# Joining two 64-row products into one 128-row product in the last inner tile of a shared feed-forward layer

## Chip, cores and metric

One core of one Trainium2 chip runs the whole program. The time is device microseconds of one execution. Before the change three runs took 1123.83, 1128.89 and 1127.62 us; the median is 1127.62 us.

## What is computed

Two residual steps on x of shape (4, 2048, 256), that is 8192 tokens of 256 channels. The first is a dynamic convolution over 31 taps, the second a feed-forward layer made of routed experts (16 experts, the best 2 for each token) and of a shared layer that every token passes. The change lies in the shared layer:

```python
SHARED_FF = 704
shared = jax.nn.silu(x @ shared_w_gate.T) * (x @ shared_w_up.T) @ shared_w_down.T
shared = shared * jax.nn.sigmoid(x @ shared_gate_w.T)
...
out = expert_out + shared
...
x = x + _layernorm(_L0_ffn_ref(_layernorm(x, axis=-1), ...), axis=-1)
```

The 704 inner channels are five tiles of 128 and one of 64.

## The kernel before, in words

The program has five blocks, one behind the other: `attention`, `routing`, `shared_and_scatter`, `experts` and `shared_and_combine`. Below, **stage 1** is `shared_and_scatter` (from about 435 us of the span), **stage 2** is `experts`, **stage 3** is `shared_and_combine` (from about 877 us to the end).

The shared layer is the class `Shared`. Its 16 chunks of 512 tokens are split between stage 1 and stage 3, 8 chunks each (`SHARED_CHUNKS`). A chunk walks six inner tiles, m = 0 to 5 (`FT` = 6). For one tile:

- TensorE, `gate_up`: 12 products of 512 columns (6 for m = 5, whose 64 gate and 64 up rows share one bank). Each 32-bit operand is held as a high and a low part, so every product is made of three: high x high, high x low, low x high.
- ScalarE, `silu`, then VectorE, `gated` (tile `hf`, the hidden values), then ScalarE again (tile `hh`, the high part), then VectorE, `hidden_low` (tile `hl`, the low part: hf minus hh).
- TensorE, `down`: for each of four groups of 128 tokens the three products hh x dh, hh x dl, hl x dh, 256 columns each (`dh`, `dl`: high and low part of the down weights). The contraction runs over the tile's rows: 128, and 64 (`FL`) in the tile m = 5. All six tiles of a chunk are summed up in one pair of banks.

`products` writes TensorE's order out by hand: `gate_up` of tile m + 2 (for the last two tiles that of the next chunk) stands ahead of `down` of tile m. So `down` of m = 5 stands between `gate_up` of tiles 1 and 2 of the next chunk. In the last chunk of a stage it is TensorE's last work there.

What stands around it: `leave` (ScalarE, L870) takes the finished chunk out of the banks, in stage 1 to DRAM. Also in stage 1, GpSimd scatters token rows with 128 indirect DMAs (L985). In stage 3 GpSimd gathers two expert rows for each token (L1271, 16 indirect DMAs a chunk) and works out the layer norm's scales (`scales`, L1278 to L1284) between them. VectorE adds expert rows and shared rows (`sums`, L1344 to L1355) at fixed places in its chunk: the sums of one half of the tokens (v = 1) of a chunk at m = 1 and 2 of the next, those of the other half at m = 4 and 5. ScalarE normalizes (L1302), VectorE adds the residual (L1362).

Of the kernel before, what the change touches and what calls it, by code (L numbers as in the profile page):

```python
# [7 lines left out]
F32 = mybir.dt.float32  # L8
# [3 lines left out]
ALU = mybir.AluOpType  # L12
# [4 lines left out]
P = 128  # L17
BATCH, SEQ, C = 4, 2048, 256
# [13 lines left out]
FF, E, MF = 704, 16, 128  # L32
FT = 6
FL = FF - (FT - 1) * P
# [786 lines left out]
class Shared:  # L821
# [67 lines left out]
    def hidden_low(self, ve, i, q, m):  # L889
        f, k, g = self.size(m), m % 2, (m + FT * q) % 4  # L890
        ve.wait_ge(self.s["hh_ok"], (self.base + i) * FT + m + 1)
        self.nc.vector.tensor_tensor(self.hl[0:f, g], self.hf[0:f, k], self.hh[0:f, g].bitcast(F32), ALU.subtract  # L892
                                     ).then_inc(self.s["hl_ok"], 1)

    def gate_up(self, pe, i, q, m):
# [14 lines left out]
    def down(self, pe, i, q, m):  # L910
        g, f = (m + FT * q) % 4, self.size(m)
        pe.wait_ge(self.s["hl_ok"], (self.base + i) * FT + m + 1)
        for t in range(4):
            o = self.pb[4 + 2 * q + t // 2][:, (t % 2) * C:(t % 2 + 1) * C]
            for j, (a, w) in enumerate(((self.hh, self.dh), (self.hh, self.dl), (self.hl, self.dh))):
                ins = self.nc.tensor.matmul(o, a[0:f, g, t * P:(t + 1) * P], w[0:f, m, :],  # L916
                                            start=(m == 0 and t % 2 == 0 and j == 0), stop=(m == FT - 1 and j == 2),
                                            skip_group_check=True)
        if m == FT - 1:
            ins.then_inc(self.s["dn_full"], 1)  # L920

# [126 lines left out]
def experts(nc, sems, eh, el, yt, ynt_d, first_d, xg_d, yg_d, ident, ones, block_expert, pb):  # L1048
    NBK = NBLK + 1
    with ExitStack() as ctx:  # L1050
# [64 lines left out]
        def _(pe):  # L1115
# [37 lines left out]
            def down(b, r):  # L1153
# [6 lines left out]
                ins.then_inc(s["y_full"], 1)  # L1160
            load_experts(0)
            steps(pe, lambda n, r: parts(n, r, (2, turn_x), (-1, turn_h), (1, gate_up), (-2, down), (2, find)), enter)

        @block.scalar
# [242 lines left out]
def _layouts(i):  # L1407
    import numpy as np
    taps = i["L0_attn_w_lin"].reshape(HEADS, KS, C)
    ring = np.concatenate([taps, taps[:, KS - 1:]], 1)[:, [(k - 1) % J for k in range(2 * J)]]  # L1410
    ring = ring.reshape(HEADS, 2 * J, HS, NG, HC).swapaxes(3, 4).reshape(HEADS, 2 * J, C)
    wd = ring.transpose(2, 0, 1).reshape(CC, P, HEADS, 2 * J).transpose(1, 0, 2, 3)
    g = np.concatenate([i["L0_ffn_gate_w"], i["L0_ffn_shared_gate_w"], np.zeros((GW - E - 1, C), "f")], 0)
    gw = g.T.reshape(CC, P, GW).transpose(1, 0, 2)
    gate, up = i["L0_ffn_shared_w_gate"], i["L0_ffn_shared_w_up"]
    rows = [a[m * P:(m + 1) * P] for m in range(FT) for a in (gate, up)]
    wsh = np.concatenate(rows, 0).T.reshape(CC, P, 2 * FF).transpose(1, 0, 2)
    dn = np.concatenate([i["L0_ffn_shared_w_down"].T, np.zeros((FT * P - FF, C), "f")], 0)
    wdn = dn.reshape(FT, P, C).transpose(1, 0, 2)
    gu = i["L0_ffn_w_gate_up"].reshape(E, CC, P, 2 * MF).transpose(0, 2, 1, 3).reshape(E, P, CC * 2 * MF)  # L1420
    we = np.concatenate([gu, i["L0_ffn_w_down"]], 2)
    named = dict(x=i["L0_attn_x"], wd=wd, gw=gw, wsh=wsh, wdn=wdn, we=we)
    return {k: np.ascontiguousarray(v) for k, v in named.items()}
# [13 lines left out]
```

## Time and profile before

| | |
|---|---|
| median of three runs | 1127.62 us (1123.83 to 1128.89) |
| span of the profiled execution | 1124.2 us (its own time is given as this span alone) |
| TensorE matmul busy | 961.3 us, 86% |
| VectorE / ScalarE / GpSimd busy | 801.2 / 574.0 / 488.8 us |
| mean granted TensorE clock | 0.933 of 2.4 GHz |
| chain that ended last | GpSimd 13%, issue 4%, TensorE 3%, others about 1% each |

How to read it: busy shares are means over stages with different limits, so the span is cut into stages first. TensorE's records overlap, because a product is listed with its whole passage through the array; what one product costs in a stream is the distance between starts of neighbours. In the chain of waits GpSimd stands first, and all of that lies in stage 3.

### The profile page before, as it was taken

The page shows a single profiled execution, that of the slowest core. Times are in us where ns is not written, and L with a number is a line of the kernel's source. Part 1 is how long each engine was busy: PE and PEld are TensorE (multiplying, and loading weights), DVE is VectorE, ACT ScalarE, POOL GpSimd, SP SyncE. Part 2 cuts the span into 40 slices and gives each one's busy share as a digit, 9 for nine tenths or more (in the row PEclk, how much of TensorE's full clock was granted, in tenths as well). Part 3 has the DMA queues.
Part 4 walks back from the last instruction along what each step waited for, and adds up shares of the span by engine and source line. Part 5 has one row for each costly group of instructions (what it writes and reads, how often), then busy time and mean ns, then how long its engine had stood idle before and what let it go on. Part 6 is the DMA issues. An engine that isn't in the chain of part 4 may idle for free. (4 is left out here: it accounts for less than half of the span.)

```text
span 1124.2 us, 28049 instructions
## 1 busy us (share of the span) xinstructions
PE 961.3 (86%) x9192; PEld 842.2 (75%) x9193; DVE 801.2 (71%) x2066; ACT 574.0 (51%) x1309; POOL 488.8 (43%) x726
## 2 busy tenths in 40 slices
PE   5997898998899505999999789999999899898881
PEld 4776787776788504888888678999898687777671
DVE  5887997787999694445444368788788378777665
ACT  5993446897254412444444345555555345444442
POOL 4322556220455342776776300000000568787774
PEclk9999998998999556999999889999999899999995
DMA  4333688532578438566665355555555546655553
GB/s 136 113 95 84 184 239 257 164 113 59 147 207 249 155 122 263 182 204 195 205 224 181 95 168 175 168 169 176 169 169 158 158 141 192 187 183 166 167 165 108
DMA packets 188966, 188.16 MB, mean 167 GB/s; under 512 B 55120, under 2 KB 169936, under 8 KB 188752
## 3 DMA queue, kind: packets, MB, share of 16 engines
q1 hardware_dynamic: 173088, 149.25, 44.2%
q0 software_dynamic: 12288, 33.57, 9.1%
q10 hardware_dynamic: 3504, 4.20, 1.2%
q8 instruction: 53, 0.87, 0.3%
q14 instruction: 33, 0.27, 0.1%
HBM read 100.81 MB, written 86.14 MB: 166 GB/s over the span
## 5 line engine op out<-in xcount | busy, mean ns | idle before, releaser
L985 POOL DMA_INDIRECT sorted_rows<-yr,sl x128 | 137.8, 1077 | 76.7 <-issue 38.0
L1271 POOL DMA_INDIRECT cy<-expert_rows,csl x128 | 139.0, 1086 | 45.3 <-issue 44.1
L606 PE MATMUL bank<-xbd,am 128*32 128x68 f32 x4096 | 138.5, 304 | 10.6 <-DMA xbd<-xn_scratch 4.7
L606 PEld LDWEIGHTS bank<-xbd,am 128*32 128x32 f32 x4096 | 122.4, 128 | 18.7 <-issue 10.5
L1264 POOL MEMSET czero<- 128x4 f32 x1 | 0.1, 101 | 241.8 <-POOLq L1050 241.8
L887 DVE TENSOR_TENSOR s_hf<-s_sg,bank 128x512 f32<-128x512 f32 (+1 forms) x48 | 33.0, 688 | 89.8 <-ACT s_sg L862 89.8
L1144 PE MATMUL bank<-eh,xh 128*128 x288 | 94.7, 329 | 0.4 <-DVE xl L1188 0.4
L1188 DVE TENSOR_TENSOR xl<-bank,xh 128x256 fp32r<-128x256 f32 x144 | 61.1, 424 | 40.8 <-ACT xh L1170 33.4
L1170 ACT ACTIVATE xh<-bank 128x256 fp32r<-128x256 f32 x144 | 55.3, 384 | 65.5 <-PE bank L1120 65.2
L407 DVE TENSOR_TENSOR am<-probs,mask 128x512 f32<-128x512 f32 x128 | 80.0, 687 | 8.4 <-ACT probs L501 7.5
L1144 PE MATMUL bank<-el,xh 128*128 x288 | 82.5, 287 | 0.0
L1144 PE MATMUL bank<-eh,xl 128*128 x288 | 82.4, 286 | 0.0
L864 ACT ACTIVATE c_hh<-c_hf 128x512 fp32r<-128x512 f32 (+1 forms) x48 | 30.4, 632 | 98.5 <-DVE c_hf L887 98.5
L916 PE MATMUL bank<-dh,c_hh 128*128 128x256 f32 (+1 forms) x192 | 57.7, 300 | 25.1 <-DVE c_hl L892 25.1
L322 POOL TENSOR_TENSOR rstd<-mv,eps 128x2 f32<-128x2 f32 (+1 forms) x68 | 14.1, 208 | 147.8 <-DVE mv L397 90.1
L1120 PE MATMUL bank<-ident,xg 128*128 128x128 f32 x288 | 57.4, 282 | 24.1 <-issue 12.5
L905 PE MATMUL bank<-c_yh,gh 128*128 128x512 f32 x176 | 71.8, 408 | 6.3 <-DVE c_yl L879 6.3
L515 ACT ACTIVATE av<-av,shift,rstd 128x256 f32<-128x256 f32 x64 | 35.0, 594 | 79.9 <-POOL shift L327 79.9
L905 PE MATMUL bank<-s_yh,gh 128*128 128x512 f32 x176 | 71.5, 406 | 4.5 <-DVE s_yl L879 4.5
L348 POOL TENSOR_TENSOR x<-av,xr 128x256 f32<-128x256 f32 x64 | 46.9, 754 | 62.5 <-ACT yn L524 59.2
L905 PE MATMUL bank<-c_yl,gh 128*128 128x512 f32 x176 | 70.5, 401 | 0.0
L905 PE MATMUL bank<-s_yl,gh 128*128 128x512 f32 x176 | 70.5, 400 | 0.0
(196 smaller groups left out, 3133.1 us busy)
## 6 DMA issues: line engine op xcount, KB each, us to landing
xg<-sorted_rows SPq DMA_DIRECT2D x144, 128.0 KB, 2.1
expert_rows<-yo SPq DMA_DIRECT2D x144, 128.0 KB, 1.8
xbd<-xn_scratch SPq DMA_DIRECT2D x128, 72.0 KB, 2.3
xt<-x SPq DMA_DIRECT2D x32, 256.0 KB, 3.0
xn_scratch<-xn SPq DMA_DIRECT2D x64, 128.0 KB, 2.7
xr<-x SPq DMA_DIRECT2D x32, 256.0 KB, 3.5
x_scratch<-x SPq DMA_DIRECT2D x32, 256.0 KB, 3.6
yn_scratch<-yn SPq DMA_DIRECT2D x32, 256.0 KB, 3.7
```

Of the source, the lines that this page charges most:

```text
L348: nc.gpsimd.tensor_tensor(x2[:, q, t], av[:, q, t], xr[:, q, t], ALU.add).then_inc(s["x2_ok"], 1)
L407: nc.vector.tensor_tensor(am[:, q, g], probs[:, bass.ds(i * CB, CB), g, None, :].to_broadcast([P, CB, 2, J]), mask[:, None].to_broadcast([ ...
L515: nc.scalar.activation(av[:, q, t], av[:, q, t], ACT.Identity, scale=rstd2[:, q, t:t + 1], bias=shift2[:, q, t:t + 1]).then_inc(s["z_ok"], 1)
L606: ins = nc.tensor.matmul(pso[q][t][J * b:J * b + J, g * MW:(g + 1) * MW], am[:, q, g, e, side], xbd[:, q, e + side, :, g], start=(g == 0 a ...
L905: ins = self.nc.tensor.matmul(self.pb[2 * k + half][:], w[:, c, col:col + P], y[:, q, c, :], start=(j == 0), stop=(j == 5))
L916: ins = self.nc.tensor.matmul(o, a[0:f, g, t * P:(t + 1) * P], w[0:f, m, :], start=(m == 0 and t % 2 == 0 and j == 0), stop=(m == FT - 1 a ...
L985: nc.gpsimd.indirect_dma_start(out=xg_d, out_offset=bass.IndirectOffsetOnAxis(ap=sl[:, q, t, u, k:k + 1], axis=0), in_=yr[:, t, u], in_off ...
L1120: ins = nc.tensor.transpose(px[r % 2][:, c * P:(c + 1) * P], xg[:, r, c * P:(c + 1) * P], ident[:])
L1144: ins = nc.tensor.matmul(pg[r % 2][:, 0:2 * MF], a[:, r % 2, c * P:(c + 1) * P], w[:, bass.ds(e, 1), c * C:(c + 1) * C], start=(j == 0), s ...
L1170: nc.scalar.activation(xh[:, r % 2], px[r % 2][:, 0:C], ACT.Copy).then_inc(s["xh_ok"], 1)
L1188: nc.vector.tensor_tensor(xl[:, r % 2], px[r % 2][:, 0:C], xh[:, r % 2].bitcast(F32), ALU.subtract).then_inc(s["xl_ok"], 1)
L1271: nc.gpsimd.indirect_dma_start(out=y[:, v, k, j], out_offset=None, in_=yg_d, in_offset=bass.IndirectOffsetOnAxis(ap=sl[:, v, k, j:j + 1], ...
```

## The change

In the tile m = 5 `hidden_low` writes the low part not to rows 0 to 63 of `hl` but to rows 64 to 127 of `hh`, below the high part. The host puts the last 64 rows of the down weights a second time where zeros were, so that rows 64 to 127 of `dh` hold the same weights as rows 0 to 63. One product over 128 rows then gives hh x dh + hl x dh; the product hh x dl over 64 rows remains, and comes first.

```diff
     def hidden_low(self, ve, i, q, m):
...
-        self.nc.vector.tensor_tensor(self.hl[0:f, g], self.hf[0:f, k], self.hh[0:f, g].bitcast(F32), ALU.subtract
+        low = self.hl[0:f, g] if m < FT - 1 else self.hh[FL:2 * FL, g]
+        self.nc.vector.tensor_tensor(low, self.hf[0:f, k], self.hh[0:f, g].bitcast(F32), ALU.subtract
...
     def down(self, pe, i, q, m):
...
-            for j, (a, w) in enumerate(((self.hh, self.dh), (self.hh, self.dl), (self.hl, self.dh))):
-                ins = self.nc.tensor.matmul(o, a[0:f, g, t * P:(t + 1) * P], w[0:f, m, :],
-                                            start=(m == 0 and t % 2 == 0 and j == 0), stop=(m == FT - 1 and j == 2),
-                                            skip_group_check=True)
+            terms = ((self.hh, self.dh, f), (self.hh, self.dl, f), (self.hl, self.dh, f))
+            if m == FT - 1:
+                terms = ((self.hh, self.dl, FL), (self.hh, self.dh, 2 * FL))
+            for j, (a, w, rows) in enumerate(terms):
+                ins = self.nc.tensor.matmul(o, a[0:rows, g, t * P:(t + 1) * P], w[0:rows, m, :],
+                                            start=(m == 0 and t % 2 == 0 and j == 0),
+                                            stop=(m == FT - 1 and j == len(terms) - 1), skip_group_check=True)
...
-    dn = np.concatenate([i["L0_ffn_shared_w_down"].T, np.zeros((FT * P - FF, C), "f")], 0)
+    dn = np.concatenate([i["L0_ffn_shared_w_down"].T, i["L0_ffn_shared_w_down"].T[FF - FL:]], 0)
```

TensorE's order in stage 1 at the end of a chunk, `down` of m = 5, the first of the four token groups with its neighbours, before (bank3 belongs to `gate_up`, bank4 takes the `down` products; the column at the end is the output's shape):

```order
L905 MATMUL bank3<-s_yl,gh 128x512
L905 MATMUL bank3<-s_yh,gl 128x512
L916 MATMUL bank4<-dh,s_hh 128x256
L916 MATMUL bank4<-dl,s_hh 128x256
L916 MATMUL bank4<-dh,s_hl 128x256
```

and with the change, the first two token groups:

```order
L906 MATMUL bank3<-s_yl,gh 128x512
L906 MATMUL bank3<-s_yh,gl 128x512
L920 MATMUL bank4<-dl,s_hh 128x256
L920 MATMUL bank4<-dh,s_hh 128x256
L920 MATMUL bank4<-dl,s_hh 128x256
```

Each of the four token groups goes from three products, all over 64 rows, to two: `dl` over 64 rows, then `dh` over 128. So `down` of m = 5 goes from 12 products of one height to 8 whose height changes at every step. Nothing ahead of it or behind it moves.

VectorE's order around the same place, before (the 64-row tile is m = 5; `el` are expert weights), and with the change:

```order
L887 TENSOR_TENSOR s_hf<-s_sg,bank2 64x512
L1032 TENSOR_TENSOR el<-eraw,eh 128x768
L892 TENSOR_TENSOR s_hl<-s_hf,s_hh 64x512
```

```order
L887 TENSOR_TENSOR s_hf<-s_sg,bank2 64x512
L1036 TENSOR_TENSOR el<-eraw,eh 128x768
L893 TENSOR_TENSOR s_hh<-s_hf,s_hh 64x512
```

The low part now goes into `s_hh`; the place in the order and the shape stay.

## Rows read from the trace of the kernel before

**Rows 1.** Windows by stage: us, busy us (instructions) by engine, clock, DMA share, GB/s.

```profile
435.20:632.64 197.44, 197.41 (x1104) 170.10 (x1104) 88.44 (x151) 87.88 (x147) 137.82 (x128) 0.98 0.60 196
...
876.60:1106.10 229.50, 204.38 (x1104) 173.00 (x1104) 164.32 (x413) 99.98 (x187) 173.37 (x211) 0.96 0.55 169
1106.10:1124.20 18.10, 0.00 (x0) 0.00 (x0) 8.22 (x24) 5.58 (x12) 4.21 (x13) 0.52 0.38 123
```

**Rows 2.** Waits, whole span: us in total, times, longest us.

```profile
PE bank L916 <- DVE c_hl L892: 25.1, 12, 7.7
...
POOL crstd L1278 <- DVE cmv L1355: 17.4, 3, 8.8
...
PE bank L905 <- DVE s_yl L879: 4.5, 1, 4.5
```

**Rows 3.** Timeline of TensorE, stage 1, boundaries of equal height: start, us, line, tiles.

```profile
461.72 0.39 PE L905 MATMUL bank<-s_yh,gl 128*128 128x512 f32 x1
461.95 0.28 PE L916 MATMUL bank<-dh,s_hh 128*128 128x256 f32 x1
...
463.26 0.28 PE L916 MATMUL bank<-dh,s_hl 128*128 128x256 f32 x1
463.38 0.40 PE L905 MATMUL bank<-s_yh,gh 128*128 128x512 f32 x1
```

**Rows 4.** Timeline of TensorE, the first `down` of m = 5 and its neighbours.

```profile
465.94 0.40 PE L905 MATMUL bank<-s_yh,gl 128*128 128x512 f32 x1
466.27 0.38 PE L916 MATMUL bank<-dh,s_hh 64*128 64x256 f32 x1
466.49 0.28 PE L916 MATMUL bank<-dl,s_hh 64*128 64x256 f32 x1
...
467.68 0.28 PE L916 MATMUL bank<-dh,s_hl 64*128 64x256 f32 x1
...
468.22 0.40 PE L905 MATMUL bank<-s_yl,gh 128*128 128x512 f32 x1
```

**Rows 5.** Timeline of TensorE weight loads at the same place.

```profile
466.26 0.18 PEld L916 LDWEIGHTS bank<-dh,s_hh 64*128 64x128 f32 x1 [0.37 <-issue]
...
467.88 0.19 PEld L905 LDWEIGHTS bank<-s_yh,gh 128*128 128x128 f32 x1
```

**Rows 6.** Timeline of TensorE, the last such pair of boundaries (stage 3).

```profile
1075.16 0.40 PE L905 MATMUL bank<-c_yh,gl 128*128 128x512 f32 x1
...
1075.71 0.28 PE L916 MATMUL bank<-dl,c_hh 64*128 64x256 f32 x1
...
1076.91 0.27 PE L916 MATMUL bank<-dh,c_hl 64*128 64x256 f32 x1
...
1077.45 0.40 PE L905 MATMUL bank<-c_yl,gh 128*128 128x512 f32 x1
```

**Rows 7.** Timeline of GpSimd, stage 3: the scales that waited.

```profile
903.90 0.77 POOL L1278 TENSOR_TENSOR crstd<-cmv,eps 128x2 f32<-128x2 f32 x2 [8.80 <-DVE cmv L1355]
...
918.25 0.77 POOL L1278 TENSOR_TENSOR crstd<-cmv,eps 128x2 f32<-128x2 f32 x2 [1.04 <-DVE cmv L1355]
...
1116.01 0.34 POOL L1278 TENSOR_TENSOR crstd<-cmv,eps 128x2 f32<-128x2 f32 x2 [7.57 <-DVE cmv L1355]
```

**Rows 8.** Timeline of ScalarE, stage 3: the first chunk leaves, and the last.

```profile
909.07 1.57 ACT L870 ACTIVATE cso<-bank,shgate 128x256 f32<-128x256 f32 x4 [3.23 <-PE bank L916]
...
1110.45 1.53 ACT L870 ACTIVATE cso<-bank,shgate 128x256 f32<-128x256 f32 x4
```

**Rows 9.** Timeline of VectorE, stage 3: 64-row low part, wait in chunk 1.

```profile
903.78 0.68 DVE L892 TENSOR_TENSOR c_hl<-c_hf,c_hh 64x512 fp32r<-64x512 f32 x1
...
911.15 0.69 DVE L887 TENSOR_TENSOR c_hf<-c_sg,bank 128x512 f32<-128x512 f32 x1 [4.59 <-ACT c_sg L862]
```

**Rows 10.** Windows in stage 3 around an idle TensorE; columns as in rows 1.

```profile
1067.00:1069.00 2.00, 0.00 (x0) 0.00 (x0) 1.94 (x8) 0.00 (x0) 1.48 (x2) 1.00 0.31 86
1069.00:1073.00 4.00, 3.30 (x14) 3.23 (x15) 3.90 (x13) 2.60 (x6) 3.16 (x3) 0.57 0.40 100
```

## Prediction, before the change was run

> **What bounds the kernel now.** The stages come first, because the shared layer runs in two of them and they have different limits. In stage 1 TensorE is busy for 197.41 of 197.44 us [rows 1]. Such a busy sum alone proves little, since listed products overlap; so the list of waits comes next. It holds for stage 1 a single wait of TensorE, 4.5 us on the first chunk's input, and none at `down`, whose waits (25.1 us in 12) all name the tiles of stage 3 [rows 2]. So in stage 1 every product starts as soon as TensorE can take it: time added to TensorE's stream there lengthens the stage one for one, and time taken out shortens it. No other engine comes near (GpSimd 137.82, VectorE 88.44, ScalarE 87.88 us).
>
> In stage 3 GpSimd sets the pace. Its three waits for VectorE's statistics (17.4 us, [rows 2]) lie at 903.90, 918.25 and 1116.01 [rows 7]: 8.80 + 1.04 + 7.57 us are all of them. Between 918.25 and the last one it waits for no other engine, while TensorE waits 25.1 us for tiles that come late. What TensorE loses in that stretch is taken out of those waits.
>
> **What one product costs, and what a change of height costs.** Durations of listed products don't add up; distances between starts do. Over 64 rows the starts at 466.49 and 467.68 are ten products apart: 0.119 us each [rows 4]. At boundaries where both neighbours contract over 128 rows, the next start comes 0.23 us after a 512-column product (461.72 to 461.95) and 0.12 us after a 256-column one (463.26 to 463.38), so going from one line to the other costs nothing [rows 3].
>
> At m = 5 it costs something in both directions. From the last 128-row product (465.94) to the second 64-row one (466.49) it is 0.55 us, where 0.23 + 0.12 would be without a loss: 0.20 us lost. From the last 64-row product (467.68) to the second 128-row one (468.22) it is 0.54 us, where 0.12 + 0.23 would do: 0.19 us lost [rows 4]. The last such pair, in stage 3, reads the same: 0.55 and 0.54 us [rows 6]. The weight loads show why: the load of the new height starts only at 466.26 (after 0.37 us without a load) and at 467.88, which is 0.32 and 0.20 us after the start of the product ahead and so 0.08 to 0.09 us after that product's own share of the stream (0.23 and 0.12 us) [rows 4, 5]. I call such a step a switch and take 0.195 us for it. The Trainium skill ("TensorEngine Tiling (Array Packing)", Tiling Modes, Key Properties) states that a change of tiling mode, unlike a change of tile, drains the engine. The trace agrees as far as it goes: a loss of 0.19 to 0.20 us at each change of height, none elsewhere.
>
> **The change part by part.**
> - *TensorE, a chunk with a successor.* Before: 12 products, 2 switches (in, out). After: 8 products, order 64, 128, 64, 128 and so on, so one switch in, seven inside, none out: 8. Removed: 4 x 0.119 = 0.48 us. Added: 6 x 0.195 = 1.17 us. Net +0.69 us.
> - *TensorE, up to the last product of m = 5* (which counts where `leave` follows, and in a stage's last chunk). Before: 11 distances of 0.119 = 1.31 us. After: 7 of 0.119 + 0.195 = 2.20 us. Net +0.89 us.
> - *Bounds of a switch.* The trace shows no 256-column stream whose height changes at every product. Lower bound: half is hidden, 0.10 us, giving +0.12 and +0.22 us. Upper bound: the next load waits for the listed end of a product (0.28 us after its start, instead of about 0.20), so 0.275 us, giving +1.17 and +1.45 us. I take 0.195, since 64 to 128 rows behind a 256-column product is just what row 467.68 shows, and the other direction differs by 0.01. That no switch inside the group costs anything is the first rival.
> - *Stage 1:* 7 x 0.69 + 0.89 = +5.7 us, all on the path (bounds 1.1 and 9.6).
> - *Stage 3, before GpSimd takes over.* ScalarE's first `leave` waits for the first chunk's last `down` (909.07, [rows 8]); behind it in its queue stands the `silu` that VectorE awaits at 911.15 [rows 9], then come the sums that GpSimd awaits at 918.25. So +0.89 us reaches GpSimd once (bounds 0.2 and 1.5).
> - *Stage 3, later.* Six more chunks at +0.69 us are 4.1 us, against 25.1 us of waits at `down`: nothing. Were those waits gone, the 4.1 us would appear. In the last chunk TensorE is done at 1106.1 [rows 1], and `leave` stands until 1110.45 behind GpSimd's scales [rows 8]: 0.89 us is hidden by 4 us.
> - *VectorE's low part to rows 64 to 127.* Same shape, same place in the queue, 0.68 us [rows 9], so nothing. If writing to other rows than it reads doubled it, in stage 1 it would be seen only in the last chunk, where TensorE is right behind: +0.7 us. A gain I exclude, since nothing is taken away. The doubled weights replace zeros: same transfers, same instructions. The new rows of `hh` bring no wait; `down` waits for the same count as before.
>
> Sum: 5.7 + 0.9 = +6.6 us (0.6%); with both bounds +1.3 and +11.1. The profiled span is 1124.2 us, 3.4 us (0.3%) under the median; as the sum is a difference, I add it to the median: 1127.6 + 6.6 = **1134.2 us**.
>
> **Rivals.**
> - *A: the height of a product doesn't matter inside a group (not slower).* Place: the eight products of m = 5. If consecutive products into the same banks stream whatever their height, the six extra switches cost nothing and four products go: -0.48 us in each of 8 chunks of stage 1, and once before GpSimd takes over: -4.3 us, **1123.3 us**. It decides from a switch price under 4 x 0.119 / 6 = 0.08 us; above that the change loses. For it: boundaries of equal height cost nothing [rows 3]. Against: both measured switches cost over twice that, each in another direction. The Trainium skill ("TensorE: Matmul & The Clock Gate", Back-to-back issue gap) gives the spacing by moving columns alone, with no term for rows; the rows at the two boundaries speak against taking that rule here. Chance 0.08.
> - *B: half of a switch is hidden.* The lower bound above: **1128.9 us**. For it: where one switch follows another, the second may find part of its drain already done. Against: both directions agree. Chance 0.07.
> - *C: the clock falls.* The eight products are 8 x 0.119 = 0.95 us of stream spread over 8 x 0.314 = 2.5 us; if that cost the granted clock, as after an idle stretch, a fall would cost 4 us at 0.57, so 4 x 0.43 = 1.7 us [rows 10]. In each chunk of stage 1: 13.8 us on top, **1148 us**. Against: with no product at all from 1067 to 1069 the clock still stood at 1.00, the 2.4 GHz level, and fell only after that [rows 10]. Chance 0.04.
> - *D: the change doesn't do what it says.* TensorE's order shows 8 products for 12 at each of the 16 places, so I give this nothing.
>
> **How the numbers follow.** The forecast itself, switches at about 0.195 us each, has 0.81. The three runs spread over 5 us, so a median of a few runs can lie 2 us off; with that and the bounds it holds from about 1129 to 1141 us. The range is 1128 to 1141: it takes in B and the upper bound (1138.7) with some room and leaves out A, C and the forecast's tails, under 2 in 10. A difference within 0.5% (5.6 us) is about what a measurement of this kernel can't tell from none, and +6.6 us is just past it. So of the forecast's 0.81 I give 0.55 to slower and 0.26 to same; B goes to same (0.07), A to same (0.06) and faster (0.02), C to slower (0.04). Rounded: slower 0.59, same 0.39, faster 0.02.
>
> **What would show it.** In TensorE's timeline of stage 1: eight products at m = 5, starts about 0.31 us apart instead of 0.12, and each weight load beginning behind the product ahead instead of during it; directly after the last one, `gate_up` without a loss; each chunk of stage 1 0.69 us and the stage 5.7 us longer, stage 2 unchanged, GpSimd's wait near 918 about 0.9 us longer, and TensorE's waits at `down` in stage 3 shorter. If the eight starts lie 0.12 us apart, A holds; about 0.22, B; a granted clock below 1.00 in mid stage 1, C. If the low part's duration leaves 0.68 us, or the last wait of GpSimd grows, a step I put at nothing was wrong.

## The result and the profile after

The change is slower by 0.43%: the ratio to the kernel before is 1.0043, 95% interval 1.0033 to 1.0054, with medians of 1131.51 us (18 runs, 1129.03 to 1135.02) and 1126.58 us (18 runs). That is +4.9 us where +6.6 was forecast: inside the range (1128 to 1141 us), on the forecast side, and short of the 0.5% that was set as the bound of "slower". The profiled execution took 1129.95 us, with a span of 1128.2 us.

First TensorE's timeline of the changed kernel at the first m = 5 of stage 1 (start us, us, engine, line, tiles), which answers to [rows 4]:

```profile
467.76 0.40 PE L906 MATMUL bank<-s_yh,gl 128*128 128x512 f32 x1
468.09 0.38 PE L920 MATMUL bank<-dl,s_hh 64*128 64x256 f32 x1
468.40 0.38 PE L920 MATMUL bank<-dh,s_hh 128*128 128x256 f32 x1
468.71 0.38 PE L920 MATMUL bank<-dl,s_hh 64*128 64x256 f32 x1
...
469.96 0.38 PE L920 MATMUL bank<-dl,s_hh 64*128 64x256 f32 x1
470.27 0.39 PE L920 MATMUL bank<-dh,s_hh 128*128 128x256 f32 x1
470.50 0.40 PE L906 MATMUL bank<-s_yh,gh 128*128 128x512 f32 x1
```

Eight products, 0.31 us from start to start (468.09 to 470.27 is seven steps, 0.311 us each; 0.314 was forecast). The last is 128 rows high. `gate_up` follows 0.23 us behind it (470.27 to 470.50), where 0.12 would be without a loss: about half of a switch is paid one step late, in the step behind the first product of the new height, as in [rows 4] (466.27 to 466.49 is 0.22 us). The weight loads, which answer to [rows 5], begin one by one behind the product ahead:

```profile
468.09 0.18 PEld L920 LDWEIGHTS bank<-dl,s_hh 64*128 64x128 f32 x1 [0.37 <-issue]
468.40 0.19 PEld L920 LDWEIGHTS bank<-dh,s_hh 128*128 128x128 f32 x1
468.71 0.18 PEld L920 LDWEIGHTS bank<-dl,s_hh 64*128 64x128 f32 x1
```

The windows by stage (columns as in [rows 1]) and the waits ([rows 2], [rows 7]) of the changed kernel:

```profile
437.15:640.13 202.98, 202.86 (x1072) 169.45 (x1072) 89.62 (x151) 88.36 (x147) 133.85 (x128) 0.99 0.58 190
882.49:1112.10 229.61, 210.18 (x1072) 171.59 (x1072) 165.30 (x413) 99.74 (x187) 173.80 (x216) 0.96 0.56 171
```

```profile
PE bank L920 <- DVE c_hl L893: 18.3, 11, 7.4
...
POOL crstd L1282 <- DVE cmv L1359: 17.0, 3, 7.6
```

```profile
909.46 0.90 POOL L1282 TENSOR_TENSOR crstd<-cmv,eps 128x2 f32<-128x2 f32 x2 [7.56 <-DVE cmv L1359]
...
924.72 0.62 POOL L1282 TENSOR_TENSOR crstd<-cmv,eps 128x2 f32<-128x2 f32 x1 [1.90 <-DVE cmv L1359]
...
1120.02 0.34 POOL L1282 TENSOR_TENSOR crstd<-cmv,eps 128x2 f32<-128x2 f32 x2 [7.58 <-DVE cmv L1359]
```

Stage 1 is 202.98 us long, against 197.44 before [rows 1]: +5.5, where +5.7 was forecast. GpSimd's second wait is 1.90 us, against 1.04 [rows 7]: +0.86, where +0.89 was forecast; the way from its first wait to its second grew by 0.9 us (909.46 to 924.72, against 903.90 to 918.25). Up to here the sum holds. But from the second wait to the third it is 195.30 us now (924.72 to 1120.02), and was 197.76 (918.25 to 1116.01): 2.5 us came back, in the stretch in which GpSimd waits for nobody and in which the forecast stood at nothing. The experiments had to show whether this is scatter, TensorE's doing, or something else that the change moved. Stage 2, which was expected unchanged, is 1.5 us shorter too: 242.75 us from TensorE's last product of stage 1 to its first of stage 3, and 244.25 before.

### The profile page after: what moved, and what is told of

It is laid out like the page before. It is cut to its first block and busy times, and to the rows that moved or that the text cites. A ratio compares the mean times of both kernels' runs of the same rounds, so it can differ in the third digit from the quotient of the medians.

```text
span 1128.2 us, 27921 instructions
## 1 busy us (share of the span) xinstructions
PE 972.3 (86%) x9128; PEld 840.6 (75%) x9129; DVE 803.0 (71%) x2066; ACT 574.3 (51%) x1309; POOL 483.2 (43%) x726
## 2 busy tenths in 40 slices
DMA packets 188965, 188.14 MB, mean 167 GB/s; under 512 B 55120, under 2 KB 169936, under 8 KB 188752
## 5 line engine op out<-in xcount | busy, mean ns | idle before, releaser
L989 POOL DMA_INDIRECT sorted_rows<-yr,sl x128 | 133.9, 1046 | 85.2 <-issue 38.0
L1275 POOL DMA_INDIRECT cy<-expert_rows,csl x128 | 136.1, 1063 | 45.3 <-issue 44.1
L920 PE MATMUL bank<-dh,c_hh 128*128 128x256 f32 x192 | 60.2, 313 | 18.3 <-DVE c_hl L893 18.3
L906 PE MATMUL bank<-c_yh,gl 128*128 128x512 f32 x176 | 70.6, 401 | 0.0
```

What stands on the lines that cost most here:

```text
L906: ins = self.nc.tensor.matmul(self.pb[2 * k + half][:], w[:, c, col:col + P], y[:, q, c, :], start=(j == 0), stop=(j == 5))
L920: ins = self.nc.tensor.matmul(o, a[0:rows, g, t * P:(t + 1) * P], w[0:rows, m, :], start=(m == 0 and t % 2 == 0 and j == 0), stop=(m == FT ...
L989: nc.gpsimd.indirect_dma_start(out=xg_d, out_offset=bass.IndirectOffsetOnAxis(ap=sl[:, q, t, u, k:k + 1], axis=0), in_=yr[:, t, u], in_off ...
L1275: nc.gpsimd.indirect_dma_start(out=y[:, v, k, j], out_offset=None, in_=yg_d, in_offset=bass.IndirectOffsetOnAxis(ap=sl[:, v, k, j:j + 1], ...
```

## The experiments

Two theories for the price in stage 1: a change of height costs 0.195 us wherever it stands (theory 1), or the joined product is dear in itself (theory 2). For stage 3: scatter, TensorE's different load (theory T), or VectorE's instruction for the low part (theory V, formed after the first eight runs). Every ratio is to the kernel before, run on the same chip.

In the tables, "period" is the distance of two neighbouring m = 5 groups in the middle of stage 1; "paced" is the time from GpSimd's second scales of stage 3 (918.25 before) to those behind its last gather (1106.19 before), 187.94 us in the first profile of before and 185.47 in that of the change. Both come from starts in the profile's timelines.

| kernel | ratio (95%) | period, us | paced, us |
|---|---|---|---|
| before, first profile | 1 | 24.31 | 187.94 |
| before again | 0.9995 (0.998 to 1.0009) | 24.31 | 188.10 |
| the change | 1.0043 (1.0033 to 1.0054) | 24.98 | 185.47 |
| the change again | 1.0045 (1.0028 to 1.0062) | 24.98 | 186.65 |
| grouped by height | 0.9949 (0.9936 to 0.9963) | 23.83 | 184.43 |
| both over 128 rows | 0.9904 (0.989 to 0.9919) | 23.43 | 186.31 |
| before, padded to 128 | 0.9976 (0.9966 to 0.9987) | 23.90 | 187.19 |
| before, twelve switches | 1.025 (1.0219 to 1.0281) | 26.24 or 27.75 | 187.49 |
| change in stage 1 alone | 1.0038 (1.0022 to 1.0055) | 24.98 | 187.72 |
| change in stage 3 alone | 0.9988 (0.9976 to 1.0) | 24.31 | 186.88 |
| before, low part to other rows | 0.9986 (0.9971 to 1.0002) | 24.31 | 186.13 |
| change, low part first | 1.0055 (1.0035 to 1.0075) | 24.98 | 189.03 |
| before, two idle copies | 0.9985 (0.997 to 1.0) | 24.31 | 188.14 |
| both over 128, two idle copies | 0.9905 (0.9885 to 0.9925) | 23.43 | 185.22 |

**Before again.**

> The kernel before, unchanged, for a second profile beside the others of this group. It shows how far stages that nobody touches move from profile to profile: stage 2 (244.25 us from TensorE's last product of stage 1 to its first of stage 3 in the first profile of before, 242.75 in that of the change) and the stretch of stage 3 in which GpSimd sets the pace (187.94 us from its second wait for statistics to its last gather's scales, 185.47 with the change). If the shortfall of the change against the forecast (4.9 us measured for 6.6) is scatter of profiles, these two stretches come out anywhere between or around those values here; if the change itself shortens them, they come out at 244.2 and 187.9 again, within 0.3 us. Time: ratio 1.000.

Stage 2 took 244.57 us and the paced stretch 188.10. So in the paced stretch the kernel before repeats itself within 0.2 us, in stage 2 within 0.3.

**Grouped by height.** All four 64-row products, then all four joined ones:

```diff
-        for t in range(4):
-            for j, (a, w, rows) in enumerate(terms):
+        order = [(t, j) for j in range(2) for t in range(4)]
+        for t, j in order:
```

> The change, with its eight products of tile m = 5 grouped by height: the four over 64 rows first, then the four over 128. Theory 1 (a change of height costs 0.195 us wherever it stands): 2 switches as before the change, 4 products of 0.119 us fewer: -0.48 us in each of 7 chunks of stage 1, -0.28 us in its last, -0.28 us ahead of GpSimd's pace in stage 3, in sum -3.9 us against before, ratio 0.9965. Starts 0.12 us apart but for one step of 0.31. Theory 2 (the joined product itself is dear, since its operand is written half by ScalarE and half by VectorE and its accumulation follows another height into the same bank; each pair costs 0.63 us whatever stands beside it): same cost as the change in its own order, ratio 1.004, starts at the four joined products 0.31 us or more apart.

Its timeline merges products of one height (x4):

```profile
468.01 0.74 PE L922 MATMUL bank<-dl,s_hh 64*128 64x256 f32 x4
468.68 0.74 PE L922 MATMUL bank<-dh,s_hh 128*128 128x256 f32 x4
469.26 0.39 PE L906 MATMUL bank<-s_yh,gh 128*128 128x512 f32 x1
```

From 468.01 to 468.68 is 0.67 us. The steps are 0.22, 0.12, 0.12 and 0.21 us, then 0.22 and 0.12: the one switch inside the group is spread over two steps, 0.21 and 0.22, and is not the single step of 0.31 that was expected; in sum it costs 0.19 us. The joined products stream like any other once they stand next to each other. The period fell by 0.48 us, as theory 1 has it, and theory 2 is out. The same eight products, with their order changed and nothing else, turn +0.43% into -0.51%. The total, -5.7 us, is more than the 3.9 expected; the paced stretch is short here too.

**Both over 128 rows.** The change with one number altered, so that the second copy of the weights' low part is used too (the small product low x low is added):

```diff
-                terms = ((self.hh, self.dl, FL), (self.hh, self.dh, 2 * FL))
+                terms = ((self.hh, self.dl, 2 * FL), (self.hh, self.dh, 2 * FL))
```

> The change, with the product with the weights' low part over all 128 rows too. Rows 64 to 127 of those weights are a copy of rows 0 to 63, so the product low x low is added, which the kernel before leaves out. No change of height is left. Theory 1: 8 products of 0.119 us and no switch, in place of 12 and 2: -0.87 us a chunk in 7 chunks of stage 1, -0.67 us in its last, -0.67 us ahead of GpSimd's pace in stage 3: -7.4 us against before, ratio 0.9934, all starts 0.12 us apart and 0.23 us behind the 512-column product. Theory 2 (joined products dear in themselves): eight products at 0.31 us, ratio 1.004 or more.

```profile
466.14 0.28 PE L920 MATMUL bank<-dl,s_hh 128*128 128x256 f32 x1
466.26 0.27 PE L920 MATMUL bank<-dh,s_hh 128*128 128x256 f32 x1
466.37 0.28 PE L920 MATMUL bank<-dl,s_hh 128*128 128x256 f32 x1
...
466.96 0.28 PE L920 MATMUL bank<-dh,s_hh 128*128 128x256 f32 x1
467.08 0.39 PE L906 MATMUL bank<-s_yh,gh 128*128 128x512 f32 x1
```

All steps are 0.12 us, and there is no loss at either end. The period is 0.88 us shorter than before (0.87 expected). Median 1115.45 us, -0.96%: of all kernels of this study, this and its variant below are the fastest. The total, 10.6 us less, is more than the 7.4 expected, and its interval leaves 7.4 out. In the profile stage 1 is 7.8 us shorter from first to last product (6.8 expected), stage 2, which the edit does not touch, 1.4 us (242.85 for 244.25), the paced stretch 1.6 us. Stage 1 begins at the lower clock here for 3.4 us, before for 6.1 us; why stage 2 is shorter is not shown.

**Before, padded to 128.** Only the height changes; the added weight rows are zeros:

```diff
     def down(self, pe, i, q, m):
-        g, f = (m + FT * q) % 4, self.size(m)
+        g, f = (m + FT * q) % 4, P
```

> The kernel before with its 12 products of tile m = 5 made over 128 rows instead of 64: the weights' rows 64 to 127 are zero there, and the other operand holds what an earlier tile left, so the sum is the same. Nothing is removed or moved, only the height is. Theory 1: the two switches of each chunk go: -0.39 us in each of 7 chunks of stage 1, -0.2 us in its last, -0.2 us in stage 3: -3.1 us, ratio 0.9972. Theory 3 (what stands at the two boundaries is not the height but the wait for the tile or the turn from one line to the other): unchanged, ratio 1.000, 0.55 and 0.54 us at the boundaries as before.

The period falls by 0.41 us (0.39 expected), the time by 2.7 us with an interval of 1.5 to 3.8 (3.1 expected). Contracting over more rows saves time here, and theory 3 is out: the loss at the two boundaries is the height.

**The change again.**

> The changed kernel, unchanged, for a second profile and beside the next three on one chip. Time: ratio 1.003 to 1.006 as before. Stretches: stage 1 from TensorE's first to its last product 202.6 us again, within 0.1, as TensorE alone sets it; stage 2 and the stretch of stage 3 that GpSimd paces anywhere within 2 us of the first profile (242.75 and 185.47 us) if their scatter has nothing to do with the change.

Time, stage 2 (243.89 us) and paced stretch lie where they were expected; the stretch is 1.2 us longer than in the first profile. Stage 1 missed: 201.23 us from first to last product, not 202.6. The difference lies in its first chunk. In the first profile the clock stood at 0.50 from 437.15 to 440.40 and at 0.56 up to 443.40, here it was at 1.00 from 439.00 on: some 1.4 us of scatter that belongs to the start of a stage. Against the kernel before (197.13 us, at the lower clock for its first 6.1 us) stage 1 is longer by 5.5 us in the first profile and by 4.1 us in this one. All six full periods read 24.98 in both.

**Before, twelve switches.**

```diff
+                rows = f if (t * 3 + j) % 2 == 0 else P
-                ins = self.nc.tensor.matmul(o, a[0:f, g, t * P:(t + 1) * P], w[0:f, m, :],
+                ins = self.nc.tensor.matmul(o, a[0:rows, g, t * P:(t + 1) * P], w[0:rows, m, :],
```

> The kernel before with its 12 products of tile m = 5 alternately over 64 and 128 rows (zero weights in the added rows, so the sum is the same): 12 switches a chunk in place of 2, no joined product, no product removed. Theory 1: +1.95 us in each of 7 chunks of stage 1, +2.15 us in its last, +2.15 us ahead of GpSimd's pace in stage 3, the rest hidden in TensorE's waits there: +18 us, ratio 1.016 (up to 1.019 if the waits of stage 3 can't take all of 1.95 us a chunk). Starts 0.31 us apart. Theory 2 (joined products dear in themselves): none here, so no more than a few us, ratio under 1.005. If GpSimd's stretch of stage 3 gets shorter when TensorE works more slowly beside it, it gets shorter here by more than with the change (187.9 us in the profile of before, 185.5 with the change).

The steps are 0.31 us and two of the six periods 26.24 us: +1.93, where +1.95 was expected. But the other four are 27.7 to 27.8 us, and the total is 1.025, beyond the 1.016 to 1.019 expected. The windows of its stage 1 (columns as in [rows 1]; the third number from the end is the granted clock) around two of the groups show the reason:

```profile
466.20:470.00 3.80, 3.80 (x14) 2.28 (x14) 1.38 (x2) 1.23 (x2) 2.98 (x3) 1.00 0.96 337
470.00:473.20 3.20, 3.20 (x17) 2.66 (x17) 0.00 (x0) 1.81 (x5) 2.32 (x3) 1.00 0.66 250
492.50:496.00 3.50, 3.50 (x13) 2.04 (x12) 1.38 (x2) 1.23 (x2) 2.89 (x3) 1.00 0.66 247
496.00:499.20 3.20, 3.20 (x9) 2.63 (x9) 0.00 (x0) 1.57 (x4) 2.29 (x4) 0.50 0.52 164
```

After the group at 466 the clock stays at 1.00, after the next one it is at 0.50, the 1.2 GHz level, in all of the 3.20 us shown: 1.5 us lost (27.75 for 26.24), at four of the six places. This is rival C, at twelve switched products; at the change's eight, the clock reads 1.00 in every 20 us window from 470 to 610 us. GpSimd's stretch is 187.49 us: a slower TensorE alone doesn't shorten it.

**The change in one stage alone.**

```diff
+        self.joined = base == 0
...
-            if m == FT - 1:
+            if m == FT - 1 and self.joined:
```

(with `base != 0` for stage 3; `hidden_low` accordingly.)

> The change in stage 1 alone; stage 3 as before. Theory 1: TensorE paces stage 1 alone, so all of +5.5 us (202.6 for 197.1 us) stays: ratio 1.0049. If part of it is given back later (something in stage 2 or 3 that waited for a fixed time), less than 1.0035.

> The change in stage 3 alone; stage 1 as before. Theory 1: +0.9 us, paid once ahead of GpSimd's pace, the rest hidden: ratio 1.0008. If slower products of TensorE relieve GpSimd's gathers, as the two profiles could suggest (187.94 against 185.47 us), about -1.5 us: ratio 0.9985.

Stage 1 alone: +0.38%, 4.3 us (2.5 to 6.2); +5.5 us lies inside the interval. Stage 3 alone: -0.12%, -1.4 us (-2.7 to 0); the two expectations were +0.9 and -1.5 us. So the gain belongs to stage 3 and comes with the change there. In all five profiles with the low part under the high part in stage 3, the paced stretch is 184.4 to 186.9 us; in the five without it 187.2 to 188.1 (five profiles each, the repeats included). The 0.3 us between the groups is small beside the 2.5 us by which the first one scatters. TensorE's load can't be what divides them, since it is lighter than before in the padded kernel and heavier in that with twelve switches, and both stand on the long side.

What does divide them is seen beside one gather. VectorE and GpSimd in the timeline of stage 3, before (start us, us):

```profile
956.66 0.17 DVE L1330 COPY csl<-slots 128x8 uint32 x1
...
956.74 0.68 DVE L892 TENSOR_TENSOR c_hl<-c_hf,c_hh 64x512 fp32r<-64x512 f32 x1
956.83 1.40 POOL L1271 DMA_INDIRECT cy<-expert_rows,csl  x1 [0.30 <-issue]
```

and with the change:

```profile
963.04 0.17 DVE L1334 COPY csl<-slots 128x8 uint32 x1
...
963.22 0.95 POOL L1275 DMA_INDIRECT cy<-expert_rows,csl  x1 [0.30 <-issue]
...
963.25 0.70 DVE L893 TENSOR_TENSOR c_hh<-c_hf,c_hh 64x512 fp32r<-64x512 f32 x1
```

Before, the low part starts 0.09 us ahead of the end of the copy in front of it, and so 0.09 us ahead of a gather, which then takes 1.40 us. With the change it starts 0.04 us behind that copy's end and 0.03 us behind the gather's start, and the gather takes 0.95 us. Over all eight chunks of a stage the distance to the end of the instruction ahead is -0.09 to -0.08 us before and +0.03 us with the change, in stage 1 as well. In four of the eight chunks of stage 3 this turns the order of low part and gather.

The last chunk shows that the instruction behind the low part moves too. Before:

```profile
1103.68 0.65 DVE L892 TENSOR_TENSOR c_hl<-c_hf,c_hh 64x512 fp32r<-64x512 f32 x1
1103.90 2.26 POOL L1271 DMA_INDIRECT cy<-expert_rows,csl  x1 [0.30 <-issue]
1104.26 1.42 DVE L1362 TENSOR_TENSOR co<-cff,cx 128x256 f32<-128x256 f32 x4
```

With the change:

```profile
1107.20 0.68 DVE L893 TENSOR_TENSOR c_hh<-c_hf,c_hh 64x512 fp32r<-64x512 f32 x1
1107.31 1.40 POOL L1275 DMA_INDIRECT cy<-expert_rows,csl  x1 [0.30 <-issue]
1107.92 1.43 DVE L1366 TENSOR_TENSOR co<-cff,cx 128x256 f32<-128x256 f32 x4
```

The gather starts behind the low part in both. Before, the next instruction on VectorE starts 0.08 us ahead of the low part's end, and the gather takes 2.26 us; with the change it starts 0.03 us behind that end, and the gather takes 1.40 us. Beside the low parts of the eight chunks stand seven gathers: 10.52 us in sum before, 8.09 us with the change. The same sum reads 10.5 us in all five profiles without the low part under the high part, and 7.6 to 8.1 us in all five with it, so it divides them far more clearly than the stretch does. These 2.4 us are the size of what came back in the first profile; in the second they are the same 2.4 us, and the paced stretch is only 1.3 to 1.5 us shorter than in the two profiles of before, so other work of GpSimd took part of it again. Four more runs tested this theory V.

**Before, low part to other rows.** It is written to rows 64 to 127 of `hl`, which nobody reads; the sum goes without the low part of this tile.

```diff
+        low = self.hl[0:f, g] if m < FT - 1 else self.hl[FL:2 * FL, g]
-        self.nc.vector.tensor_tensor(self.hl[0:f, g], self.hf[0:f, k], self.hh[0:f, g].bitcast(F32), ALU.subtract
+        self.nc.vector.tensor_tensor(low, self.hf[0:f, k], self.hh[0:f, g].bitcast(F32), ALU.subtract
```

> The kernel before, with VectorE's low part of tile m = 5 written to rows 64 to 127 of its own tile hl instead of rows 0 to 63; TensorE still reads rows 0 to 63, so the low part of this tile is left out of the result. TensorE's stream, all waits and all counts are those of before; only the rows that one VectorE instruction writes differ. Theory V (the change's time in stage 3 comes from this instruction: it starts 0.12 us later than before, 0.03 us behind the end of the copy ahead of it instead of 0.09 us before that end, and so comes just behind instead of just ahead of the start of one of GpSimd's gathers, which then takes 0.95 us instead of 1.40): the 0.12 us and the short gathers appear here too, GpSimd's paced stretch falls from 187.9 to about 186.2 us, ratio 0.9985. Theory T (it comes from TensorE's fewer products): nothing changes, ratio 1.000, four gathers still 1.40 us beside the low part.

```profile
956.74 0.17 DVE L1331 COPY csl<-slots 128x8 uint32 x1
...
956.92 0.94 POOL L1272 DMA_INDIRECT cy<-expert_rows,csl  x1 [0.30 <-issue]
956.94 0.70 DVE L893 TENSOR_TENSOR c_hl<-c_hf,c_hh 64x512 fp32r<-64x512 f32 x1
```

With TensorE as before, only the rows of one output differ, and both signs appear: the start behind the copy's end and the short gather, in the same four chunks. The paced stretch is 186.13 us. The ratio is what theory V expected, though its interval just reaches 1, so that the time alone does not exclude theory T; the starts and the gathers do.

**The change, low part first.** The copy of row numbers goes behind the low part:

```diff
                     if m == 5:
                         sums(0, i, (2, 3))
-                        if not last:
-                            find(0, i + 1)
                     sh.hidden_low(ve, i, q, m)
+                    if m == 5 and not last:
+                        find(0, i + 1)
```

> The change, with VectorE's small copy of the next gathers' row numbers in stage 3 placed behind the low part of tile m = 5 instead of ahead of it. TensorE as in the change. Theory V: the low part starts about 0.1 us ahead of the gather again, the gathers beside it take 1.40 us again, GpSimd's paced stretch is back at 187.5 to 188 us, and the change costs 1.5 to 2 us more than it does: ratio 1.0055 to 1.0065 against before (1.0043 for the change). Theory T: no difference from the change, 1.0043, stretch at 185.5 to 186.7.

```profile
964.41 0.69 DVE L893 TENSOR_TENSOR c_hh<-c_hf,c_hh 64x512 fp32r<-64x512 f32 x1
964.51 1.41 POOL L1275 DMA_INDIRECT cy<-expert_rows,csl  x1 [0.30 <-issue]
```

The low part is 0.10 to 0.11 us ahead of the gather again, in seven chunks, and all seven gathers take 1.40 or 1.41 us, as theory V has it. The paced stretch, 189.03 us, is back to the long side, but 1 us beyond the 187.5 to 188 expected; what adds this is not shown. The ratio, +0.55%, is at the lower end of what theory V expected, and its interval (1.0035 to 1.0075) also holds the change's own 1.0043, so the time does not separate the theories; the gathers and the stretch, 185.5 to 186.7 us by theory T, do.

**Two idle copies**, in the kernel before and in the variant with both products over 128 rows:

```diff
                         if not last:
                             find(0, i + 1)
+                        for j in range(2):
+                            nc.vector.tensor_copy(pad[:, 2 * q + j], slots[:, 0:G, :])
                     sh.hidden_low(ve, i, q, m)
```

> The kernel before, with two idle copies of 8 numbers on VectorE in stage 3 right ahead of the low part of tile m = 5; nothing else. They delay the low part by some 0.16 us, so that it starts behind the gather's start (-0.06 us) instead of 0.10 us ahead of it. Theory V: work added, time gained: four or more gathers fall from 1.40 to 0.95 us, the paced stretch from 187.9 to about 186 us, ratio 0.9985. Theory T: ratio 1.000 or slightly above.

> The variant of the change with all eight products over 128 rows, and with the same two idle copies in stage 3. Theory V: there the low part still starts 0.05 to 0.10 us ahead of a gather in two chunks of the eight, which take 1.40 to 1.46 us; a further 0.16 us puts it behind the gather in these too, so about 0.9 us less than the variant alone (0.9904): ratio 0.9896. Theory T: as the variant, 0.9904 or slightly above.

In the kernel before the copies do what was expected to the order: the low part starts 0.04 to 0.05 us behind the gather in four chunks, which takes 0.95 or 0.96 us. The ratio is 0.9985, but its interval reaches 1 and the profiled stretch, 188.14 us, is not shorter: among other losses the gather beside the last chunk's low part, 2.26 us before, took 2.74 here. So this run is inconclusive on the time. In the fast variant the gathers beside the low part are all short, 0.94 to 0.96 us, and the paced stretch is 1.1 us shorter than without the copies (185.22 for 186.31), where 0.9 was expected. Yet the time is 0.9905, no better than 0.9904 without the copies; the 0.9896 expected lies inside the interval, so the time decides nothing.

## Why the prediction was right, and where it was off

- *The price of a switch* was right, and with it the likeliest case. 0.195 us was read from two boundaries of the kernel before; the change's period grew by 0.67 us (0.69 forecast), and the edits with two, no, no and twelve switches moved it from that of before by -0.48, -0.88, -0.41 and, where the clock stayed, +1.93 us (expected -0.48, -0.87, -0.39, +1.95). A detail of its sign was wrong: `gate_up` does not follow the last product without a loss, since 0.10 us of the last switch lies there; the sum of eight switches is the same. Rival A is out: steps of 0.31 us, not 0.12. Rival B too: 0.22 us would have been the step.
- *Stage 1* came out at +5.5 us (5.7) in the first profile and, with its clock up some 3 us sooner, at +4.1 in the second; *GpSimd's delayed entry* at +0.9 us (0.89). TensorE's waits at `down` in stage 3 fell from 25.1 to 18.3 us, which is more than the 4.1 us that were to be taken out of them.
- *The step that failed* is "VectorE's low part to rows 64 to 127: same shape, same place in the queue, so nothing", with its sentence "A gain I exclude, since nothing is taken away". The instruction's duration did stay (0.70 for 0.68 us), but its start moved by 0.12 us, in four chunks past the start of a gather, and the start of the instruction behind it moved too, which shortened a fifth gather. In the first profile of the change the paced stretch is 2.5 us shorter than before, in the second 1.4 us; the change in stage 3 alone measures -1.4 us in all, with the +0.9 us of the delayed entry in it. With the first profile's stage 1, 5.5 + 0.9 - 1.4 to 2.5 = +3.9 to +5.0 us, and +4.9 was measured; with the second's it is +2.5 to +3.6. The sum leaves out stage 2, which was 1.5 and 0.7 us shorter in the two profiles of the change than in those of before; no run shows whether the change has a part in that.
- That the change "doesn't do what it says" (D) got no chance, and rightly. The clock (C) did not fall at eight switched products; that the mechanism exists was seen only at twelve.
- The chances: 0.59 for slower by over 0.5% hung on a sum only 1 us beyond that bound. One unseen term of -2 us was enough to bring the result under it. That the time still fell into the range is owed to the range's width, which was set for the price of a switch and not for a gain in stage 3. Of the 2.7 us between the 1134.2 us forecast and the 1131.5 measured, 1.0 lies in the kernel before, whose median went from 1127.62 us in three runs to 1126.58 in 18.

## What to carry to other kernels

Where products of different contraction heights stand in one stream, count the changes of height before counting the products: here 0.195 us each is more than the 0.119 us of a 256-column product. Group them by height, or pad the short ones with zero (or useful) rows; here one altered number turned a loss of 0.43% into a gain of 0.96%. And when an instruction's output moves to other partitions, its start can move even if its duration doesn't: look at what begins within 0.1 us of it on an engine that shares something with it.

## What the runs showed of the hardware

- *VectorE starts an instruction later when its output begins at other rows than the output before.* By 0.11 to 0.12 us, in all 16 chunks of the change, and likewise where only the output's rows were changed. The instruction behind it, which writes from row 0 again, moves as well: in seven chunks of stage 1 from 0.08 us ahead of the low part's end to 0.03 us behind it. The Trainium skill ("VectorE: DVE Perf Modes", Two Vector instructions with no wait between them) gives such a rule: an instruction is held until all earlier ones have finished if its output starts in another quadrant of partitions than the last output did. The trace agrees: 0.03 us behind the end of the one ahead instead of 0.08 to 0.09 us before it.
- *Who starts first decides whether a gather is slow.* A gather that starts 0.02 to 0.05 us ahead of the low part took 0.94 to 0.96 us, one that starts 0.09 to 0.11 us behind it took 1.40 or 1.41 us. Wherever the low part was first and the next VectorE instruction did not overlap it, the gather ended 0.82 or 0.83 us behind the low part's end, whether it had started 0.03 or 0.18 us behind its start; so it lasts as long as it has to wait. One place is otherwise: in the kernel with both products over 128 rows a gather listed 0.04 us behind the low part took 0.95 us, and the low part 0.76. The Trainium skill ("SBUF — State Buffer", SBUF: two separate sides) describes the port pair that VectorE and GpSimd share as an exclusive lock for a whole instruction: of a VectorE instruction with two SBUF inputs, as the low part has, and a GpSimd one that reads SBUF, whichever starts first holds it and blocks the other. The rows agree in their order; that the port is the cause was not shown, only that the order is.
- *TensorE's clock can fall while TensorE is listed as busy throughout.* In the kernel with twelve switched products it stood at the 1.2 GHz level in the 3.20 us shown right behind such a group, at four of six places, while the profile lists TensorE as busy for 3.50 of 3.50 us ahead of the fall; at a loss of 1.5 us each time.
